# Dispatch without the identity products in front of its first six tiles

## The reference, cut to what matters

```python
xn = _l2norm(x, axis=2)
phin = scale * _l2norm(phi, axis=0)
logits = jnp.einsum('bmd,dnp->bmnp', xn, phin)
d = jax.nn.softmax(logits, axis=1)
c = jax.nn.softmax(logits.reshape(b_, m_, n_ * p_), axis=-1).reshape(b_, m_, n_, p_)
xs = jnp.einsum('bmd,bmnp->bnpd', xn, d)
h = jax.nn.gelu(jnp.einsum('bnpd,ndh->bnph', xs, w1) + b1[None, :, None, :], approximate=False)
ys = jnp.einsum('bnph,nhd->bnpd', h, w2) + b2[None, :, None, :]
y = jnp.einsum('bnpd,bmnp->bmd', ys, c)
```

## Time and profile before

| | us |
|---|---|
| median of 3 runs | 979.98 |
| fastest and slowest of them | 979.36, 984.73 |
| profiled execution, its own time | 982.76 |
| its span, first to last instruction | 980.9 |

### The profile page before, as it was taken

The page is one execution under the profiler, slowest core; times in us unless marked ns, Lnnn a source line. Parts: engine busy times, 40 slices in busy tenths (PEclk is TensorE's granted clock), DMA queues, the critical chain, the costliest instruction groups (busy, mean ns, idle before and its releaser), DMA issues. The chain is left out here.

```text
span 980.9 us, 17879 instructions
## 1 busy us (share of the span) xinstructions
PE 858.5 (88%) x6209; PEld 621.5 (63%) x6209; DVE 455.5 (46%) x1520; ACT 318.1 (32%) x904; POOL 280.1 (29%) x242
## 2 busy tenths in 40 slices
PE   6899999899999999893997999977465999999991
PEld 6787888676466655463854777757453666666661
DVE  6864565548443322241654688836781222222220
ACT  2544333237433332240042566633101121221210
POOL 1540000000000000000233455530027488888444
PEclk9999999799899999996997899985556999999996
DMA  8992000270089999982500000002005354455222
GB/s 265 281 329 97 2 2 2 81 305 2 23 320 423 423 422 423 425 263 70 175 1 1 1 2 0 1 2 53 24 24 140 79 105 104 92 101 104 39 24 25
DMA packets 59881, 128.93 MB, mean 131 GB/s; under 512 B 26334, under 2 KB 42256, under 8 KB 50112
## 3 DMA queue, kind: packets, MB, share of 16 engines
q1 hardware_dynamic: 29858, 118.61, 33.3%
q0 software_dynamic: 29952, 9.36, 7.0%
HBM read 115.76 MB, written 11.49 MB: 130 GB/s over the span
## 5 line engine op out<-in xcount | busy, mean ns | idle before, releaser
L1831 POOL DMA_INDIRECT out_dram<-yr,put x48 | 105.7, 2203 | 58.3 <-issue 35.4
L1286 POOL MEMSET xg<- 96x74 f32 x1 | 0.2, 157 | 406.9 <-PE bank L1259 406.9
L1818 POOL DMA_INDIRECT zr<-z_rows,take x48 | 66.6, 1388 | 84.6 <-issue 84.6
L1895 PE MATMUL bank<-zTa,w 128*128 128x372 f32 x256 | 90.0, 496 | 0.8 <-DVE zTb L1969 0.8
L1978 DVE TENSOR_TENSOR hT<-sg,bank 128x372 f32<-128x372 f32 x64 | 31.8, 538 | 107.5 <-ACT sg L1939 63.1
L1895 PEld LDWEIGHTS bank<-zTa,w 128*128 128x128 f32 x256 | 47.5, 194 | 38.2 <-ACT sg L1939 8.4
L1143 DVE COPY eh<-bank 128x384 f32<-128x384 f32 x32 | 17.8, 558 | 110.6 <-PE bank L1181 110.6
L1909 PE MATMUL bank<-w2r,hT 128*124 128x192 f32 x384 | 66.1, 329 | 0.8 <-DVE hT L1978 0.8
L1939 ACT ACTIVATE sg<-bank 128x372 f32<-128x372 f32 x64 | 27.3, 478 | 115.4 <-PE bank L1900 115.4
L1909 PEld LDWEIGHTS bank<-w2r,hT 128*124 128x124 f32 x384 | 61.9, 187 | 3.8 <-issue 3.8
L1327 POOL TENSOR_TENSOR nl<-nl,nr 111x1036 f32<-111x1036 f32 x22 | 42.1, 1914 | 61.7 <-DVE nr L1437 61.7
(11 more groups left out here) (298 smaller groups left out, 1798.4 us busy)
## 6 DMA issues: line engine op xcount, KB each, us to landing
w1l<-in_w_dram SPq DMA_DIRECT2D x20, 1152.0 KB, 16.3
w2l<-in_w_dram SPq DMA_DIRECT2D x20, 1152.0 KB, 16.9
w1s<-in_w_dram SPq DMA_DIRECT2D x12, 1152.0 KB, 15.5
w2s<-in_w_dram SPq DMA_DIRECT2D x12, 1152.0 KB, 15.1
w<-in_w_dram SPq DMA_DIRECT2D x8, 1024.0 KB, 8.0
xt<-in_x_dram SPq DMA_DIRECT2D x22, 336.0 KB, 8.0
xT<-in_xT_dram SPq DMA_DIRECT2D x22, 333.0 KB, 7.4
w2r<-in_w2r_dram SPq DMA_DIRECT2D x8, 384.0 KB, 4.1
```

Of the source, the lines that this page charges most:

```text
L1818: nc.gpsimd.indirect_dma_start(zr[b][:, j, :], None, z_rows, bass.IndirectOffsetOnAxis(ap=take[:, k:k + 1], axis=0), bounds_check=NROW - 1 ...
L1831: nc.gpsimd.indirect_dma_start(rows_out, bass.IndirectOffsetOnAxis(ap=put[:, k:k + 1], axis=0), yr[e % 2][:, j, :], None, bounds_check=OUT ...
L1895: nc.tensor.matmul(bank[to + 2 * part + half][:, 0:HS], w13[b][:, 0, at:at + 128], zTa[b][:, half * HS:(half + 1) * HS], start=True, stop= ...
```

## The change

The function `dense` and its seven uses in dispatch go, and with them the wait for the weights that it read. Nothing is put in their place. The similar products in the near stage (L1496) stay.

```diff
-        def dense(times, to):
-            for _ in range(times):
-                nc.tensor.matmul(bank[to][:, 0:256], ident, w1s[0][:, 0:256], start=True, stop=True)
-
         def dispatch_pe(pe):
-            pe.wait_ge(s_w1[0], 16)
             pe.wait_ge(s_ph, 1)
             pe.wait_ge(s_brg, T)
             for c in range(2):
                 last = nc.tensor.matmul(bank[7][0:HALF, 0:NE], ones[0:HALF, 0:HALF], phisq[:, c, :], start=(c == 0), stop=(c == 1))
             last.then_inc(s_phn, 1)
-            dense(12, 5)
             pe.wait_ge(s_ph, 5)
 
             def transpose_x(t, q):
                 b = q % 2
-                if isinstance(t, int) and t < 6:
-                    dense(3, 5)
                 pe.wait_ge(s_hn, T + t + 1)
                 if after(t, 1):
                     pe.wait_ge(s_hTc, T + t)
```

## The result

The changed kernel takes 1014.83 us (median of 4 runs, 1010.71 to 1018.17), the kernel before beside it 980.65 us: 1.0335 times as long, with an interval of 1.0283 to 1.0387. It is slower, as forecast, but by more: 34 us where 21.7 were said, and outside the range, which ended at 1010. The profiled execution took 1014.32 us with a span of 1012.5, 31.6 more than the profiled one of before.

What follows compares the result with a forecast made beforehand. TensorE was taken to set the pace of dispatch. With dispatch at clock 0.50 throughout, the first expert product comes at 285.1 instead of 263.37 us: 979.98 + 21.7 = 1001.7 us, range 972 to 1010.

Steps and rivals of the forecast that it cites:

- the two 20 us stretches of the earlier trace: Routing (21.10 us) and 88 products of 96 columns (20.10 us): TensorE busy almost without a gap, clock stayed at 0.50.
- Both rivals with a rise in the full turns: Dispatch clock returns after 5 us (973.7 us; 0.21 including never falling) or after 20 us (979.7 us; 0.13).
- The reason given for the clock at 195 us: At tile 0: clock already 0.50 from attention's tail, and TensorE idle some 5 us without the products, so dispatch starts at 0.50.
- The rival in which the clock never falls: Dispatch at 1.00 throughout, only the products' direct 10.3 us saved: 969.7 us, chance 0.01.
- The full turn: Dispatch, 18 turns from the logits of tile 3: 3.85 us each at 0.50, against 2.31 at 1.00.
- The thin turns: Dispatch's first turns, 0 to 3, where TensorE waits for ScalarE's copy: 2.44 us each at 0.50, full turns from 203.6 us.
- The tail: End of dispatch, from the last full turn to the first expert product: 12.2 us at 0.50.
- What follows dispatch: Weight stream and everything behind it move by the same amount as dispatch's end; nothing added for later stages.
- The upper end of the range: Dispatch at 0.50 with 4.3 us a full turn: 1010 us.
- Twice the whole turn: Upper bound for a full turn of dispatch at 0.50: 4.62 us, giving 1015.6 us, left out of the range.

Runs made afterwards that it cites:

- the burst in front of tile 5: Kernel before without the twelve products and the threes in front of the first six tiles; fifteen in one run in front of tile 5 instead: 990.98 us, 1.005.
- the narrow products: Kernel before with its products 64 instead of 256 columns wide and twice as many: three executions between 1029.89 and 1039.51 us, a fourth 982.89 us.
- the eight kernels above: Follow-up kernels, each the kernel before with edits to its identity products; four ran beside it at 984.67 us, four beside it at 982.81 us.
- the threes alone: Kernel before without the twelve products after the norms of phi; three in front of each of the first six tiles stay: 982.65 us, 0.9983.
- one in every turn: Kernel before without the twelve, with one product in front of every tile's transposes, all 22 turns: 1026.83, 1030.38, 1038.56 and 992.16 us.

## Why the prediction was right in sign and wrong in size

**The clock, right.** The forecast hung on whether the full turns would bring the clock back. They did not, for 74.5 us; the two 20 us stretches of the earlier trace rows were the right precedents, and the burst in front of tile 5 shows that it was the clock and not another engine or wait: the same turns are 4.13 us without it and 2.31 behind it. Both rivals with a rise in the full turns fall. The reason given for the clock at 195 us was only partly right: I had it at 0.50 from attention on, and in the profile after it fell later, in the wait for `xn`. The outcome at tile 0 is the same, but by luck as far as that ground goes, which changes from execution to execution: at 186 to 188 us the clock was 1.00 in seven of the ten profiles of this case, the changed kernel's among them. The rival in which the clock never falls was given 0.01 on that row; it fails because the clock fell at about 191.9 us, in the 5.38 us wait. The prediction also has the clock at 0.50 while the first twelve products run. By its rows it rose 4.0 us after they had begun, when about ten of their 24 records, five products, had started (14 records up to 194 us in the earlier trace rows, four of them L1009's); the argument does not hang on it.

**The rule of the skill.** The full turns were busy for 74.46 of 74.50 us at 0.50, the narrow products for 11.39 of 11.40 without bringing 1.00 back. The Trainium skill ("TensorE: Matmul & The Clock Gate", the part on the clock gate) tells of a clock released by sustained activity, and these traces do not agree with that if a busy engine is taken for activity; with the wide products they do.

**The full turn, mis-sized.** This is the step that failed. I had 3.85 us, a sum of 3.96 less something for L1050; it was 4.13 us, and 18 turns make 5.0 us of it. By its steps: the logits took 218.06 - 217.25 = 0.81 us and 218.99 - 218.06 = 0.93, where I had 0.67 and 0.76; `transpose_x` 0.39 (0.38), the inputs 0.81 and 0.84 (0.91 and 0.84), `transpose_d` 0.35 (0.40). The little that I took off for L1050 was right. The logits alone were 0.31 us a turn too cheap, and `transpose_d` gave 0.05 of that back. The two prices of the logits came from rows of another shape. L1009 has 96 columns of weights where L1024 has 111, and a transpose of L1636 took 0.19 us where a record of L1026 took 0.23. Both errors pointed down. At 1.00 L1032 took 0.44 and L1034 0.53 us, so their factors are 1.84 and 1.75. L1052's, 0.84 to 0.48, is 1.75 too and was known: the steps' own time by that factor would have given 0.77 and 0.93, closer than another form's time. The whole turn by it would have been 2.31 x 1.75 = 4.04 us.

**The thin turns, mis-sized for the same reason.** A thin turn was 197.89 - 195.01 = 2.88 us where 2.44 was said, and the full turns began at 204.74 in place of 203.6: 1.1 us. **The tail** was right: 291.65 - 279.15 = 12.5 us where 12.2 was said.

**What follows dispatch.** The forecast moved it as a whole. The weight stream and the experts did move with the first expert product. But 3.3 us came on top in stages whose code is unchanged, where the forecast had nothing. Whether they belong to the products is not shown. In the profiles of the eight kernels above the time that the later stages added or gave back against the profile of before lies between -4.4 us (the threes alone) and +2.2 (one in every turn), with the same code there; 3.3 is a little outside that, and there is one profile of the changed kernel. The interval of the measured ratio, 27.8 to 38.0 us, takes in the 28.3 us of dispatch alone. A forecast that is carried from one profiled execution can be off by some us at either end.

**The sum.** 5.0 + 1.1 + 0.3 us in dispatch and 3.3 us later, on 21.7, make the 31.6 us of the two profiles to 0.2. The medians stand 34.2 apart, since the profiled execution of before was 2.1 us above its median and that of the changed kernel 0.5 below. The upper end of the range took 4.3 us a turn and gave 1010, with nothing for the thin turns, the later stages or the spread of the runs. The turn as measured lies inside that end, and by itself would have put the time at 1001.7 + 5.0 = 1006.7 us; the terms that had no room took it out of the range. Twice the whole turn, 1015.6, would have held the time, but with a turn that did not occur.

## What to carry to other kernels

Products that compute nothing can carry weight. Before they are removed, or added, look at the granted clock of the stretch behind them and ask whether the work there has ever brought the clock back in the trace, not only whether it keeps it. If they stay, put them where the engine waits anyway: one wide product in each wait of the four thin turns carried the clock as three in front of the transposes did, and the kernel got 1% faster. And price a step at the lower clock by its own time at the higher one times a measured factor, not by the time of a similar instruction.

## What had not been expected of the hardware

- Busy for 11.39 of 11.40 us with records of 64 columns, TensorE lost its clock early in that stretch and did not get it back; busy for 4.70 us with records of 256 columns, it did.
- Two kernels ended in one of two ways: with narrow products, or one product in each turn, three executions of four took 1027 to 1040 us and one 983 or 992. The changed kernel and the six others had no such pairs in 4 to 12 runs each, nor had the kernel before in 17 and 19.
- The thin turns behind the twelve products, busy for 2.40 of their first 3.30 us, were enough to lose the clock within two turns of 1.9 and 2.2 us.
